# Edge messages summed by node on one Trainium2 core: rank-major places in DRAM, one load for a unit of two bins

## The reference, cut to what matters

```python
row, col = edge_index            # edges come sorted by col
h = concat([x[col], edge_attr])  # 64 + 64 features
h = relu(h @ W1.T + b1)          # 128
h = relu(h @ W2.T + b2)          # 128
summed = segment_sum(h, row, num_segments=6250)
cnt = segment_sum(ones, row, num_segments=6250)
agg = summed / maximum(cnt, 1)
z = relu(concat([x, agg, u]) @ Wa.T + ba)
out = x_in + z @ Wb.T + bb
```

## Time and profile before

| | |
|---|---|
| time, median of 3 runs | 1899.47 us (1896.35 to 1899.72) |
| time of the profiled execution | 1902.48 us |
| its span, first to last instruction | 1900.7 us |
| mean granted TensorE clock | 0.972 of full speed |
| busy: PE, DVE, ACT, POOL | 1732.0, 1340.0, 1428.0, 1509.7 us |
| DMA packets | 312,201 with 369.10 MB |

### The profile page before, as it was taken

One profiled execution on the slowest core, in us unless ns is written; L12 is line 12 of the kernel. 1 busy time (PEld: TensorE's weight loads), 2 busy tenths in 40 slices (PEclk: granted clock), 3 DMA queues, 4 the chain that ended last, 5 costly groups with the idle time before them and its releaser, 6 DMA issues.

```text
span 1900.7 us, 43131 instructions
## 1 busy us (share of the span) xinstructions
PE 1732.0 (91%) x12376; PEld 1463.0 (77%) x12376; DVE 1340.0 (71%) x4868; ACT 1428.0 (75%) x2591; POOL 1509.7 (79%) x991
## 2 busy tenths in 40 slices
PE   5898888999999999999899999999999999976828
PEld 3676777888888888888788888888888888866725
DVE  8665655777777777778677777777777777755727
ACT  4687877888888888888788888888888888842315
POOL 8488888888888888888888888888888888878850
PEclk9999999999999999999999999999999999988968
DMA  9988888999999999999899999999999999997755
GB/s 330 269 169 145 156 148 141 199 197 205 195 207 187 199 203 199 194 205 197 176 199 194 199 202 200 195 194 209 202 191 201 200 204 202 199 210 155 159 136 198
DMA packets 312201, 369.10 MB, mean 194 GB/s; under 512 B 40832, under 2 KB 196064, under 8 KB 311328
## 3 DMA queue, kind: packets, MB, share of 16 engines
q1 hardware_dynamic: 175200, 302.12, 55.1%
q0 software_dynamic: 135360, 62.15, 34.5%
q10 hardware_dynamic: 1408, 2.03, 0.3%
HBM read 203.87 MB, written 159.27 MB: 191 GB/s over the span
## 4 chain that ended last, share of the span: by engine, by line
POOL 53%; issue 20%; DMA 11%; PE 9%; ACT 3%; DVE 2%; SPq 1%; POOLq 0%; ACTq 0%; DVEq 0%
POOL sums L819 48%; DMA sums<-regA,idx 9%; POOL sums L807 5%; PE bank L1351 2%; PE bank L1400 2%; PE bank L1362 1%; DMA sums<-vscat,vidx 1%; PE bank L1374 1%; ACT h L921 1%; PE bank L1390 1%; ACT regA L929 1%; PE bank L1276 1%; PE bank L1476 1%; ACT regA L955 0%; DMA p_table<-regB 0%
## 5 line engine op out<-in xcount | busy, mean ns | idle before, releaser
L819 POOL DMA_INDIRECT sums<-regA,idx x844 | 1318.3, 1562 | 293.0 <-issue 242.6
L1351 PEld LDWEIGHTS bank<-h,regC 128*128 128x128 f32 x3072 | 387.4, 193 | 180.7 <-ACT h L940 127.8
L1351 PE MATMUL bank<-h,regC 128*128 128x130 f32 x3072 | 432.0, 284 | 64.5 <-ACT h L940 64.5
L1374 PE MATMUL bank<-regA,L 128*128 128x512 f32 x806 | 432.3, 619 | 2.8 <-DVE regA L1143 2.7
L1400 PE MATMUL bank<-w,h 128*128 128x128 f32 x3224 | 430.1, 277 | 0.0
L1400 PEld LDWEIGHTS bank<-w,h 128*128 128x128 f32 x3224 | 396.8, 194 | 1.1 <-ACT h L921 0.6
L921 ACT ACTIVATE h<-bank,b1c 128x512 f32<-128x512 f32 x403 | 275.6, 684 | 136.9 <-PE bank L1374 131.9
L1362 PE MATMUL bank<-regC 128*128 128x129 f32 x2352 | 296.9, 280 | 23.0 <-DVE regB L1130 12.7
L1390 PEld LDWEIGHTS bank<-h,regC 128*128 128x128 f32 x1688 | 218.9, 191 | 119.7 <-issue 91.3
L1362 PEld LDWEIGHTS bank<-regC 128*128 128x128 f32 x2352 | 277.4, 194 | 37.3 <-ACT vscat L961 21.9
L904 ACT ACTIVATE regC<-bank 128x520 f32<-128x520 f32 x384 | 231.8, 604 | 87.8 <-PE bank L1351 84.5
(11 more groups left out here) (143 smaller groups left out, 1526.9 us busy)
## 6 DMA issues: line engine op xcount, KB each, us to landing
regC<-slots SPq DMA_DIRECT2D x294, 260.0 KB, 5.6
regA<-in_ea SPq DMA_DIRECT2D x202, 256.0 KB
slots<-regC SPq DMA_DIRECT2D x192, 260.0 KB
src<-rows_src SPq DMA_DIRECT2D x107, 256.0 KB
slots<-regC SPq DMA_DIRECT2D x192, 138.1 KB
sums<-regA,idx POOLq DMA_INDIRECT x844
dstR<-rows_dst SPq DMA_DIRECT2D x101, 128.0 KB
sums<-zeros SPq DMA_DIRECT2D x20, 645.0 KB, 6.7
```

Of the source, the lines that this page charges most:

```text
L819: nc.gpsimd.indirect_dma_start(out=sums[k], out_offset=bass.IndirectOffsetOnAxis(ap=idx[:, n % RING, t:t + 1], axis=0), in_=scat[:, n % 4, ...
L1351: last = T.matmul(psSlot(t)[:, k, :], place, h2[:, g % 2, t, :], start=True, stop=True)
L1374: T.matmul(psL1(s % 2), L[:, s % RING, :], R[:, s % RING, :], start=True, stop=True).then_inc(l1_done, 1)
```

## The change

Places are numbered rank by rank, place = 49 * rank + bin. So for a given group and rank, neighbouring bins lie side by side in DRAM (4,160 bytes for two), and (group, rank) runs over 128 rows with one stride. A unit is loaded by one DMA of 128 rows of 4,160 bytes; a unit of one bin by one DMA of 128 rows of 2,080 bytes. `arrived` counts one load per unit. The instruction that builds `perm` (`L1152`) writes the same 784 columns with the loops of rank and bin exchanged: its PSUM operand now steps through the bins in the innermost loop and is repeated over the ranks, and the rank numbers are repeated in the innermost loop.

```diff
 def arrived(m):
-    parts = {n: unit_bins(q)[1] for (_, q), n in UNIT_NO.items()}
-    return sum(parts[n] for n in users(m))
+    return len(users(m))
@@ SP @@
                     h0 = BINNED_NO[block[0]]
-                    for i in range(nb):
-                        sp.dma_start(loaded(m)[0:CAP * len(block), i, :, :].rearrange("p t c -> p (t c)"),
-                                     slots[h0:h0 + len(block), CAP * (b + i):CAP * (b + i + 1), :]).then_inc(unit_in[buffer_of(m)], 16)
+                    side_by_side = slots[h0:h0 + len(block), :, :].rearrange("n (j b) x -> (n j) (b x)", b=NBIN)
+                    sp.dma_start(loaded(m)[0:CAP * len(block), 0:nb, :, :].rearrange("p b t c -> p (b t c)"),
+                                 side_by_side[:, b * TPG * W:(b + nb) * TPG * W]).then_inc(unit_in[buffer_of(m)], 16)
@@ DVE @@
-                    VE.tensor_tensor(perm[:, n % 2, :, OVER:PW].rearrange("p t (b j) -> p t b j", j=CAP), ranked.unsqueeze(3).broadcast_to([P, TPG, NBIN, CAP]),
-                                     ranks[:, :].unsqueeze(1).unsqueeze(1).broadcast_to([P, TPG, NBIN, CAP]), ALU.is_equal).then_inc(perm_ready, 1)
+                    VE.tensor_tensor(perm[:, n % 2, :, OVER:PW].rearrange("p t (j b) -> p t j b", b=NBIN), ranked.unsqueeze(2).broadcast_to([P, TPG, CAP, NBIN]),
+                                     ranks[:, :].unsqueeze(1).unsqueeze(3).broadcast_to([P, TPG, CAP, NBIN]), ALU.is_equal).then_inc(perm_ready, 1)
```

## The result

The changed kernel is slower: median 1908.76 us (1904.65 to 1914.47, 6 runs) against 1897.95 us, ratio 1.0061 with a 95% interval of 1.0046 to 1.0077. Run again, unaltered, it had 1911.03 us, ratio 1.0070 (1.0049 to 1.0092). The forecast was no change to be told.

The account below looks back on a forecast made before the run. POOL's own scatter pace was taken as the bound; loads, unit landing, perm and stores counted as nothing, shorter landing waits as about -2 us, so the median goes from 1899.5 to 1897.5 us; range 1889 to 1909 us.

Parts of the forecast that it names:

- The bound: POOL's scatters: 1.545 us of work each and 0.305 us between two, at their own pace 98% of the time.
- the door: How soon POOL's scatters land: the only way the change reaches the end, worth at most 10 us to the good.
- the term on the DMA engines: Double-row packets on q1 free 20 us of each engine, so scatters' landing waits shrink by a fifth: 2 us less.
- The sum: All terms for the whole kernel together: about -2 us, median from 1899.5 to 1897.5 us.
- The slower rival: On the DMA engines, double packets hold scatters up, each up to 700 ns: 1909.5 to 1914.5 us; chance 0.18.
- its sign: Sign of the slower rival in POOL's scatters: 60 or more landing waits, and longer ones.
- Loads on SP: 144 fewer loads to issue free 87 us of SP's time, which doesn't set the end: counted as nothing.
- Waits for a unit: DVE's waits for loads: two in the run, 9.5 us, none added; counted as nothing.
- `perm`: Instruction at line 1152 with its loops exchanged: same 784 elements, still about 960 ns; counted as nothing.
- the number of packets: On q1, the queue of SP's loads: some 20,700 packets less (144 x 144) with the same bytes.

Follow-up runs that it names:

- e2: Changed kernel, but each two-bin unit loaded by two DMAs of 64 neighbouring partitions each, in 4,160-byte rows; ratio 1.0040 against the kernel before.
- f2: Changed kernel, but first five blocks one DMA of 2,080-byte rows per bin, last-block units two DMAs (even, odd partitions) of 4,160-byte rows; ratio 1.0004 against kernel before.
- g1: Changed kernel, but first five blocks one DMA of 2,080-byte rows per bin, last-block units four DMAs (every fourth partition), 4,160-byte rows; ratio 0.9990 against kernel before.
- g2: Changed kernel, but each unit loaded by two DMAs, for even and odd partitions, in 4,160-byte rows; ratio 1.0023 against the kernel before.
- e8: Changed kernel, but SP reads one number into a register after each load of a two-bin unit, about 0.5 us; ratio 1.0027 against the kernel before.
- e1: Changed kernel with its new places and perm loops, but each two-bin unit loaded by two DMAs of 2,080-byte rows; ratio 1.0007 against the kernel before.
- e5: Changed kernel, but first five blocks loaded by one DMA of 2,080-byte rows per bin, last block still joined in 4,160-byte rows; ratio 1.0038 against kernel before.
- f3: First five blocks one DMA of 2,080-byte rows per bin; last-block units (bins q and q+25) one DMA of two 2,080-byte rows per partition; ratio 1.0017 against kernel before.
- e10: Kernel before, but each bin of the last block loaded by two DMAs of 1,040-byte rows; median 1895.20 us against 1898.94, ratio 0.9983.
- e6: Changed kernel's places, but each two-bin unit loaded by four DMAs of 1,040-byte rows, in all blocks; ratio 1.0008 against the kernel before.

## Why the prediction was wrong

- **The bound and the door were right.** POOL's pace is the same, and the time went through the landing of scatters: 9.3 of 10.0 us in the second profile.
- **The step that failed** is the term on the DMA engines: "if the net 10.0 us of landing waits shrink by about a fifth, 2 us go". The relief of the engines came: a share of 0.95 became 0.93 in the middle, and q1's packets took some 12 us less of each engine (0.551 x 1900.7 less 0.544 x 1902.9 us), where the sum had 20; a packet of 4,160 bytes took 203 ns on the mean of the run, where the sum had 191. Yet the waits grew to 14.0 and 19.3 us. The sum took a scatter's landing for a matter of how much the engines have to do. The runs show that it depends on the form in which the work is given: the same bytes in one, two or four DMAs per unit leave 4 to 10, 2 to 5 and at most 0.3 us of waits beside the last block (e2 aside). For the first five blocks this is inferred, not seen.
- **The slower rival had the time and the place, not the cause.** It gave 1909.5 to 1914.5 us; 1908.8 and 1911.0 were measured, and the last block, from whose rows it was priced, has half of the loss. But its mechanism, double packets, isn't borne out there: f2 and g1 have these packets in the last block without the loss. By the waits, what holds scatters up there is the joined DMA. So its number was partly luck, and so it is that the first median lies just inside the range, which reached up to 1909 us for this rival; the second lies outside. I gave the rival 0.18 because 30 waits in 940 seemed far from the edge. The count did stay small, 35 and 55, under the 60 that I had named as its sign; the waits that came were longer, up to 3.9 us.
- The Trainium skill ("DMA: Bandwidth & Descriptors", "Queues, rings and completion order") has an engine go on to another queue at the end of a packet, and counts 9 to 17 descriptors in one. I read its packet as the profile's. If its packet is a DMA's whole share on an engine, the table agrees but for e2: by the code, that share is 8 rows in one of the loads before, and twice the bytes in a joined one; e2's is no larger than g2's. The stretch of 3.2 us without a packet of q0 shows that scatters do stand back while SP's queue is served. No row shows the order within an engine, so the rule itself isn't shown.
- **Loads on SP.** "I count this as nothing" was wrong as well. SP's time does not set the end, yet giving 0.55 us per joined load back to it (e8) is worth 0.34 to 0.43%. By which transfers a sooner SP does harm wasn't found; of the 212 packets in the stretch above, 115 are of the edge features that SP issued behind the units.
- **Waits for a unit, `perm`, the number of packets**: as forecast. DVE waits 9.5 us for loads, as before; 964 against 962 ns; 154,464 packets as worked out.

Open: by what the first five blocks lose their half; whether 4,160-byte packets cost something there (g2 against e1), or in the last block when they come in one DMA (e5 against f3); and why e2 loses where f2 and g2 don't or lose less.

## What to carry to other kernels

Where the bound is a chain of small transfers, each waiting for an earlier one, try to cut a bulk transfer beside them into several DMAs before joining it into one, even if joining saves packets and issue time. Look at how many of the small transfers already land late, and where: here the cut gained in that stretch (e10), and cutting every load gained nothing (e6). One profile was not enough here: those of the changed kernel lie 8.6 us apart.

## What was not expected of the hardware

Joining saved packets, but a unit was not seen to come sooner. The profile tells the landing of only a few loads, all of the last block: 12 joined ones land 6.8 us (median) after their issue. Before, it tells that of eight loads, so four units, and the 5.6 us of the earlier trace rows stand on these; the second half of a unit had landed 6.5 us (median) after the first was issued. In e1, again four units, this takes 7.1 us. So it is not shown that one DMA with fewer packets brings a unit sooner or later.

Which partitions a DMA writes matters. e2 and g2 load the same rows of 4,160 bytes by as many DMAs; e2's write 64 neighbouring partitions, g2's every other one. SP's queue in e2 and then in g2 (packets, MB, share of 16 engines):

```profile
q1 hardware_dynamic: 156864, 302.12, 56.1%
```

```profile
q1 hardware_dynamic: 156864, 302.12, 54.8%
```

The packets and bytes are the same, but with 64 neighbouring partitions they take longer: a packet of 4,160 bytes 228 ns on the mean, with alternating ones 201 ns (from the packets of the two traces). The kernel loses 0.40% and 0.23%, with intervals that overlap. And a load of 128 rows of 2,080 bytes was issued faster from the new places: 478 ns in e1, 603 ns before. The even stride of the rows is not enough to explain it, as e2's loads, 64 rows of one stride, take 597 ns:

```profile
L628 SPq DMA_DIRECT2D regC<-slots x294: 319/478/1672, 343.0 to 1790.1; - x147
```

```profile
L628 SPq DMA_DIRECT2D regC<-slots x300: 444/597/1583, 340.7 to 1792.4; - x150
```
